# A graph kernel's gather queue: slots blanked two gathers ahead, direct rows taken two pairs later

## The reference

```python
# layer 0: maximum over the neighbours, 0 for a row without any
masked = where(adj != 0, x[None], lowest)
x = layernorm(x + where(has_neighbour, masked.max(1), 0))
# layer 1: graph attention
h = x @ W
e = leaky_relu((h @ a_src)[:, None] + (h @ a_dst)[None, :], 0.2)
valid = (adj > 0) & (h.sum(1) != 0)[None, :]
att = where(valid, softmax(where(valid, e, -1e9), 1), 0)
att = where(att >= 1e-4, att, 0) * valid.sum(1)[:, None]
x = layernorm(x + elu(h + att @ h))
```

## Time and profile before

| | |
|---|---|
| median of 3 runs | 856.14 us (855.97 to 856.28) |
| the profiled execution's own time | 856.39 us |
| its span, first to last instruction | 854.6 us |
| busy: TensorE, VectorE, ScalarE, GpSimd | 681.6, 581.6, 579.7, 359.0 us |
| gathers of direct rows, of extra rows | 160 of 1087 ns, 80 of 1154 ns on the mean |
| blanks | 240 of 219 ns |
| mean granted clock of TensorE | 0.896 |

### The profile page before, as it was taken

One profiled execution on the slowest core, in us unless ns is written; L12 is line 12 of the kernel. 1 busy time (PEld: TensorE's weight loads), 2 busy tenths in 40 slices (PEclk: granted clock), 3 DMA queues, 4 the chain that ended last, 5 costly groups with the idle time before them and its releaser, 6 DMA issues.

```text
span 854.6 us, 17555 instructions
## 1 busy us (share of the span) xinstructions
PE 681.6 (80%) x6675; PEld 518.7 (61%) x6675; DVE 581.6 (68%) x1320; ACT 579.7 (68%) x853; POOL 359.0 (42%) x534
## 2 busy tenths in 40 slices
PE   3999976966966967966966859799498989899843
PEld 1656643634634634634644439698398888899842
DVE  4657646836836836836846679883374999999683
ACT  4998773754754754754763787689137999998461
POOL 4100466666666666666566566766500000000020
PEclk9999996987987987987996969999699999999957
DMA  9997353743743843743744142231022122322030
GB/s 191 208 181 150 91 120 59 177 109 84 177 108 82 179 106 82 176 108 81 176 106 102 42 161 66 72 113 39 25 86 76 56 81 81 118 81 57 13 53 15
DMA packets 60513, 87.38 MB, mean 102 GB/s; under 512 B 7714, under 2 KB 33326, under 8 KB 60428
## 3 DMA queue, kind: packets, MB, share of 16 engines
q0 software_dynamic: 27328, 42.14, 27.4%
q1 hardware_dynamic: 33100, 44.10, 16.0%
HBM read 108.12 MB, written 21.04 MB: 151 GB/s over the span
## 4 chain that ended last, share of the span: by engine, by line
POOL 35%; issue 24%; PE 16%; DVE 11%; ACT 11%; DMA 1%; POOLq 1%; DVEq 0%; ACTq 0%
POOL G L704 20%; POOL G L712 8%; POOL G L696 6%; PE psR L1246 4%; PE psS L1056 4%; ACT x_split L873 3%; ACT adj_in L873 2%; DVE x_split L1704 2%; ACT at_home L785 2%; PE psA L1027 2%; ACT hot L792 1%; PE psR L1037 1%; PE psR L1331 1%; POOL adj_in L647 1%; DVE acc L1457 1%
## 5 line engine op out<-in xcount | busy, mean ns | idle before, releaser
L704 POOL DMA_INDIRECT G<-in_x_dram,idx x160 | 174.0, 1087 | 139.1 <-POOL G L696 95.2
L1056 PE MATMUL psS<-hot,x_split 128*128 128x512 bf16 x768 | 217.5, 393 | 15.4 <-DVE acc L1457 12.6
L1457 DVE TENSOR_TENSOR acc<-acc,psS 128x1024 f32<-128x1024 f32 x120 | 146.0, 1217 | 66.7 <-PE psS L1056 63.4
L792 ACT ACTIVATE hot<-psR,is_none 128x512 bf16<-128x512 f32 x256 | 166.5, 703 | 19.9 <-PE psR L1037 18.9
L785 ACT ACTIVATE at_home<-psA 128x1024 fp8e4<-128x1024 bf16 x128 | 133.2, 1041 | 58.9 <-PE psA L1027 55.9
L1056 PEld LDWEIGHTS psS<-hot,x_split 128*128 128x128 bf16 x768 | 75.2, 99 | 82.9 <-DVE acc L1457 15.7
L712 POOL DMA_INDIRECT G<-in_x_dram,idx_extra x80 | 92.3, 1154 | 60.6 <-POOL G L696 47.7
L1037 PE MATMUL psR<-at_home,first 128*128 128x512 fp8e4 x256 | 100.6, 394 | 3.4 <-ACT hot L792 3.3
L1071 PEld LDWEIGHTS psC<-taken_book,hot 128*128 128x128 bf16 x1024 | 61.7, 98 | 63.2 <-issue 13.4
L1027 PE MATMUL psA<-ident_bf,adj_in 128*128 128x128 bf16 x1024 | 82.1, 225 | 14.0 <-DVE taken_book L1432 10.6
L738 POOL DMA_INDIRECT adj_in<-in_adj_dram,exact_idx x4 | 5.1, 1282 | 203.7 <-DVE exact_idx L1991 202.8
(11 more groups left out here) (316 smaller groups left out, 1381.8 us busy)
## 6 DMA issues: line engine op xcount, KB each, us to landing
adj_in<-in_adj_dram POOLq DMA_DIRECT2D x28, 1024.0 KB
adjT_dram<-at_home SPq DMA_DIRECT2D x32, 512.0 KB
at_home<-adjT_dram SPq DMA_DIRECT2D x32, 384.0 KB
adj_in<-in_adj_dram POOLq DMA_DIRECT2D x8, 512.0 KB, 7.7
at_home<-adjT_dram SPq DMA_DIRECT2D x16, 256.0 KB
G<-in_x_dram,idx POOLq DMA_INDIRECT x160
own<-in_x_dram SPq DMA_DIRECT2D x8, 256.0 KB
x_dram<-x1w SPq DMA_DIRECT2D x8, 256.0 KB
```

Source lines behind the costliest of these rows:

```text
L704: pool.indirect_dma_start(out=G[:, SLOT_AT[n], :], out_offset=None, in_=x, in_offset=bass.IndirectOffsetOnAxis(ap=idx[:, t, k:k + 1], axis=0),
L792: nc.scalar.activation(hot[:, n % 4, :], psR[:, n % 2, :], ACT.Relu, bias=is_none[:, :]).then_inc(hot_ready, 1)
L1056: mm = nc.tensor.matmul(psS[:, b, s % 2 * ROWS:(s % 2 + 1) * ROWS], x_split[:, k, s, :], hot[:, n % 4, :], start=(k == 0), stop=(k == 2))
L1457: V.tensor_tensor(acc_flat, acc_flat, psS[:, b, :], ALU.max).then_inc(free[b], 1)
```

## The change

```diff
@@ -713,14 +713,15 @@
                         out=G[:, SLOT_AT[n], :], out_offset=None, in_=x,
                         in_offset=bass.IndirectOffsetOnAxis(ap=idx_extra[:, k:k + 1], axis=0),
                         bounds_check=N - 1, oob_is_err=False).then_inc(extra_gathered, 16)
-                if n + 1 < len(SLOT_AT):
-                    blank(g, n + 1)
+                if n + 2 < len(SLOT_AT):
+                    blank(g, n + 2)
 
             for g in range(GROUPS + 1):
                 load_adj(g + 1, 0)
                 load_adj(g + 1, 1)
                 if g:
                     blank(g - 1, 0)
+                    blank(g - 1, 1)
                     for n in range(DIRECT * GT // 2):
                         gather(g - 1, n)
                 load_adj(g + 1, 2)
@@ -1720,8 +1721,8 @@
                     if g >= 1:
                         if u in (0, 1, 3, 5):
                             top_keys(g - 1, (u + 1) // 2)
-                        if u in (2, 4) and g >= 2:
-                            direct_max(g - 2, u // 2 - 1)
+                        if u in (4, 6) and g >= 2:
+                            direct_max(g - 2, u // 2 - 2)
                         if u in (6, 7):
                             decode(g - 1, u - 6)
                         if u in (8, 9):
```

## The result

The changed kernel took 738.88 us (median of 4 runs, 738.44 to 741.82) against 856.06 (855.68 to 856.28) for the kernel before in the same runs: ratio 0.8639, interval 0.8616 to 0.8661. The profiled execution took 741.82 us, its span is 740.0, the granted clock 0.959 (before 0.896). It is only half of the result: the same file, run again on two other occasions, took 881 us. The experiments are mostly about that.

The account below looks back on a forecast made before the run. POOL's queue of gathers and blanks was taken as the bound, 63.8 us a group. Rounds of 49.5 us and a faster last group gain 112.8 us, less 3 for ScalarE: 856.4 - 110 = 746 us, range 728 to 782.

Parts of the forecast that it names:

- step 1: POOL's gathers: blanking two ahead shrinks the gap before each gather from 1.01 to 0.45 us, pitch 1.45 us.
- Rival B: POOL's gathers: the gap stays, pitch 2.01 us, round 63.8 us, time 856 us; chance 0.06.
- steps 2 to 4: Rounds: POOL's group 48.7 us, VectorE and TensorE 48.4 with the maximum two pairs later, coupled round taken as 49.5.
- The two charges: Rounds: 1 us added for VectorE's fullness at the maximum's new place, and a further allowance for coupled queues, reaching 49.5 us.
- POOL's own term: POOL's group of 30 gathers: 27 gaps less 0.56 us each, 15.1 us off 63.8, leaving 48.7 us.
- The last group: Last group's gathers: list starts them at 446.4, direct rows there at 485.9, VectorE arrives at 489.8 without waiting.
- the sum: Whole timeline: last list at 445.4, last extra rows at 504.4 instead of 617.2, 112.8 us gained, 110 after ScalarE's charge.
- rival C: POOL's gathers lengthen, by masks or an undrained transfer queue, giving back half the gap's gain: 795 us; chance 0.12.
- The 766 us: Estimate from the skill's shared-port lock between VectorE and GpSimd: one lock a group, 8 x 2.5 us.
- the 3 us for ScalarE: Between last round and last extras: ScalarE's slack falls from 33 to 8 us, so 3 us are added.
- rival D: Slot 20's blank before gather 19 waits for late-taken extras, delaying maximum, list and next group: 890 us; chance 0.02.
- signs of being right: Profile signs: gaps 0.3 to 0.5 us, groups 48 to 51, direct-row waits at most 3, last extras wait 4 to 6.

Follow-up runs that it names:

- The runs with and without masks: Changed kernel with one spare write and the last list earlier, 760.1 us; the same with one-column masks in attention parts 1 to 14, 753.98 us.
- B or C: Two chips on which the changed kernel was run again unaltered, against the kernel before: 881.38 us (ratio 1.0302) and 881.63 us (ratio 1.0292).
- A, B and C: The three chips of the follow-up runs; the kernel before took 854.9 us on A, 856.9 on B, 855.8 and 855.9 on C.
- 128 columns more: Changed kernel plus one spare 128-column write ahead of each blank: 794.81 us on chip A; with the last list earlier too, 760.1 us on chip C.
- the late maximum alone: Kernel before with only the direct maximum moved behind pairs 4 and 6, blanks still one ahead: 854.06 us, ratio 0.9988, chip A.

## Why the prediction was right, and where it was not

**The gap** (step 1): forecast 0.45 us, measured 0.38. The mechanism is the one named, the latency in front of a gather hides behind other work. Its form is a blank that lies whole between two gathers and 0.16 us behind it, not 0.15 + 0.30 as next to a load. Rival B, a gap that stays, is out: of the 212 gathers of the changed kernel that follow a blank and are not the first of their group, 211 start 0.16 or 0.17 us behind its end, and one 0.84.

**The round** (steps 2 to 4): 49.5 us taken, 47.7 measured. The two charges that made it longer than TensorE's 47.4, 1 us for the crowded place of the maximum and 1 for the coupling, were not there. That is 9.3 us by the end of the last round (410.50 against 419.8), and the list is 9.6 early (435.79 against 445.4). POOL's own term, 48.7, was too long as well: within the 47.9 us between the first gathers of groups 4 and 5 it still waits 2.44 us for the list, and the smaller gap alone takes 27 x 0.07 = 1.9 us off the term.

**The last group**: here the sum was too good. The gathers up to the direct rows were to take 39.5 us from the first gather on; VectorE reads the rows 46.8 us after the first gather, after a wait of 5.14 us where none was forecast. The sum had left the stretching by the masks out as one case in 240, and that was a misreading of the trace of before. It has one gather of 6.92 us, but two more above 3 us, and 38 of the 240 last over 1.1 us. Those two, and the masks that VectorE runs beside the first of them:

```profile
533.74 3.66 POOL L712 DMA_INDIRECT G<-in_x_dram,idx_extra  x1 [0.79 <-issue]
...
600.54 3.40 POOL L712 DMA_INDIRECT G<-in_x_dram,idx_extra  x1 [0.79 <-POOL G L696]
...
533.04 3.49 DVE L1704 SCALAR_TENSOR_TENSOR adj_in<-adj_in,at_home 128x1024 f32<-128x1024 f32 x3
```

In the changed kernel it is 17 of the last group's 30 gathers, most of them at 1.4 to 2.0 us, three at 3.49, 4.02 and 7.11. The group's 20 direct gathers add up to 38.9 us where they took 29.8 before: the denser queue meets more masks, as rival C said, and that takes 9 of the 12 us back that the gaps give there. The masks of that stretch, VectorE's timeline in the 739 us run:

```profile
471.52 3.49 DVE L1705 SCALAR_TENSOR_TENSOR x_split<-x_split,at_home 128x1024 f32<-128x1024 f32 x3
474.93 3.49 DVE L1705 SCALAR_TENSOR_TENSOR adj_in<-adj_in,at_home 128x1024 f32<-128x1024 f32 x3
```

They are six masks of 1.22 us without a stop. They end at 478.4, the gather of 7.11 us at 479.3. The rest of rival C's mechanism, gathers that get longer everywhere, came only in small: of the 180 gathers of groups 0 to 5, 163 take 1.00 to 1.10 us, and 17 take 1.13 to 1.58. One of these 17, with the direct maximum beside it:

```profile
363.30 1.49 POOL L712 DMA_INDIRECT G<-in_x_dram,idx_extra  x1 [0.17 <-POOL G L696]
```

The direct maximum (362.69 to 363.91 above) and the masks both have two inputs in SBUF, and each of the 17 runs beside an operation of VectorE of which that holds. The running maximum has one input in SBUF and one in PSUM; of the 88 gathers that run beside it and beside no operation of the other kind, none takes over 1.09 us. By the Trainium skill, "SBUF — State Buffer" (two separate sides), VectorE and GpSimd share a port pair that one of them locks for a whole operation, among others when VectorE's has two inputs in SBUF and GpSimd's reads SBUF. The runs with and without masks agree with it, and so does the row above. The page says nothing of a gather that is held over six operations in a row, as here. The 766 us worked out from its figures were too high, since in the rounds a meeting costs 0.1 to 0.6 us and not 2.5.

**The sum**: 9.6 us ahead at the list, 7 of them lost again in the last group, the extra rows at 501.80 against 504.4, and the 3 us for ScalarE came as 0.8. VectorE waits 5.14 us for the last direct rows and 8.29 for the last extra ones, where at most 3 and 4 to 6 were named as signs of being right. The span fell by 114.6 us where 110 were forecast. The first result is right for the reasons given, with wrong sizes of opposite sign: that 746 came so close is partly luck.

**What failed** is an assumption that no step names: that GpSimd's queue can become denser and the engines beside it keep their pace. It held in the one measurement of the first result. On the two other chips TensorE, VectorE and ScalarE fall behind during the gathers, the round is 68 us, and the kernel is 2.9 to 3.0% slower than before. Slower had a chance of 0.02, and by a mechanism (rival D) that did not come: in the 739 us run POOL does not stop between gathers 18 and 19. That the queue's empty 0.79 us might be useful to somebody else was not among the rivals, and the rows of before could not show it: at a pitch of 2.01 us nothing falls behind. So the forecast holds for the first result alone; had the same file been measured on B or C, 746 would have been off by 135 us and the sign wrong. That it was measured where it was is luck.

**Shown**: in the runs on A, B and C the loss grows as the pitch shrinks (table), it begins with the gathers and is gone some 8 us behind them, more work on POOL removes it, the bytes of the rows do not matter. **Open**: by what path POOL's gathers delay the others (their descriptors or the completions of their packets), and why the first run is free of it at 1.39 us. No run tells these apart. A chip, a placement of the program or other work on the chip that differs would do it, and identical code in the rounds (128 columns more, chips A and C) did differ by 3.5 us a round.

The version to keep is the changed kernel with one spare write of a slot ahead of each blank and the last list earlier: 760.1 us on chip C, faster than the kernel before (855.8) and the changed one (881.6) there. It was not run where the changed kernel takes 739; with rounds of 51.3 us in place of 47.7 it would be some 20 us slower there, an estimate from the two rounds and the 5 us of the list.

## What to carry to other kernels

When a helper engine's queue is the bound, its idle gaps may protect the others: after closing them, look at the other engines' instruction counts in a stretch with the queue running and in one without, and at waits whose releaser the profile cannot find. Try the pitch as a parameter, since the best one here was neither the shortest nor the old one, and confirm a gain of this kind on more than one chip before believing it. Shortening a wait (39.6 us of VectorE's in the late maximum alone) is worth nothing while another engine sets the round.

## What was not expected of the hardware

- Indirect transfers issued by GpSimd every 1.30 to 1.47 us can take TensorE from 112 to 121 matmuls in 10 us to 55 to 63, with granted clocks between 0.62 and 0.90, and lay 107.5 us of waits for no visible releaser on VectorE. At 1.53 us most or all of it is gone. The gathers themselves have the same lengths and gaps in the run that suffers and in the one that does not. TensorE's clock is back at 1.00 only some 8 us behind the last gather.
- A gather that follows an awaited write starts 0.79 us after it; one whose write was awaited two gathers ago starts 0.16 us behind the write between.
- A second 128 x 128 write behind a first costs 0.14 us, not 0.22.
- Six masks of VectorE back to back (1.22 us each) hold one gather for 7.11 us; without masks the last group's gathers take 1.03 us each instead of 1.69. Single VectorE operations with two inputs in SBUF, a maximum among them, stretch a gather from 1.00 to between 1.13 and 1.58 us.
